# First layer: adjacency pieces loaded at most three ahead of their transposes

## The reference

```python
def _L0_gnn_ref(x, A_shape, W, bias, b):
    y = jnp.linalg.norm(x, axis=-1, keepdims=True)
    A = x @ x.T / (y @ y.T)
    A = A * b
    A = jnp.tanh(A / 8.0) * 8.0
    A = jnp.exp(A) * A_shape
    A = A / jnp.sum(A, axis=-1, keepdims=True)
    x = A @ x
    return x @ W.T + bias
...
x = x + _L0_gnn_ref(_layernorm(x, axis=-1), adj, L0_gnn_W, L0_gnn_bias, L0_gnn_b)
```

## Time and profile before

| | us |
|---|---|
| median of 3 runs | 858.69 |
| lowest and highest | 857.1, 860.33 |
| the profiled execution | 859.55 |
| its span, first to last instruction | 857.8 |
| busy PE, DVE, ACT, POOL in the span | 725.4, 626.7, 450.7, 273.9 |

### The profile page before, as it was taken

One profiled execution on the slowest core, in us unless ns is written; L12 is line 12 of the kernel. 1 busy time (PEld: TensorE's weight loads), 2 busy tenths in 40 slices (PEclk: granted clock), 3 DMA queues, 4 the chain that ended last, 5 costly groups with the idle time before them and its releaser, 6 DMA issues.

```text
span 857.8 us, 15889 instructions
## 1 busy us (share of the span) xinstructions
PE 725.4 (85%) x5287; PEld 550.3 (64%) x5294; DVE 626.7 (73%) x2265; ACT 450.7 (53%) x689; POOL 273.9 (32%) x585
## 2 busy tenths in 40 slices
PE   4799999849999688999999997968678697798893
PEld 2566766529998444777777676755446585787463
DVE  6336656715444468998981799999899999999757
ACT  2366476115555145655653582849687585722153
POOL 4310422555666201112100152142250667770000
PEclk9899999879999899999999998879979898989897
DMA  9999730186887300000000000000000002001001
GB/s 155 193 173 156 136 72 16 40 213 192 231 235 205 118 1 1 1 1 2 2 2 1 1 2 2 2 1 2 0 1 1 2 2 74 26 3 32 1 2 49
DMA packets 82186, 50.37 MB, mean 59 GB/s; under 512 B 42193, under 2 KB 78929, under 8 KB 82097
## 3 DMA queue, kind: packets, MB, share of 16 engines
q1 hardware_dynamic: 64304, 28.35, 15.0%
q0 software_dynamic: 11456, 14.62, 9.1%
q10 hardware_dynamic: 6336, 6.32, 3.1%
HBM read 39.69 MB, written 9.57 MB: 57 GB/s over the span
## 4 chain that ended last, share of the span: by engine, by line
DVE 37%; PE 16%; ACT 5%; issue 5%; DVEq 1%; POOLq 1%; POOL 0%; ACTq 0%
DVE big L1602 6%; DVE cand L1366 5%; DVE cand L1520 4%; PE bank L2145 3%; PE bank L2049 3%; DVE hacc L1515 2%; DVE rm L1360 2%; DVE cand L1541 2%; DVE top L1536 2%; DVE big L1591 2%; PE bank L2128 2%; PE bank L2329 2%; DVE big L1588 2%; PE bank L2342 1%; ACT UT L1861 1%
## 5 line engine op out<-in xcount | busy, mean ns | idle before, releaser
L2128 PE MATMUL bank<-ident,big 128*128 128x128 f32 x512 | 79.6, 304 | 28.4 <-DVEq L1625 19.1
L2128 PEld LDWEIGHTS bank<-ident,big 128*128 128x128 f32 x512 | 61.2, 153 | 54.4 <-DVEq L1625 21.0
L1875 ACT ACTIVATE big<-bank 128x512 f32<-128x512 f32 x128 | 70.4, 597 | 46.6 <-PE bank L2128 46.6
L2049 PE MATMUL bank<-kk,qq 64*128 64x512 f32 x256 | 76.0, 711 | 16.8 <-ACT big L1845 16.2
L2056 PEld LDWEIGHTS bank<-parts,adjT 128*128 128x128 bf16 x1536 | 86.9, 98 | 3.2 <-issue 2.8
L2056 PE MATMUL bank<-parts,adjT 128*128 128x128 bf16 x1536 | 88.2, 219 | 0.1
L1845 ACT ACTIVATE big<-bank,negm 128x2048 f32<-128x2048 f32 x32 | 62.7, 1958 | 48.7 <-DVE fsc L1652 38.4
L1602 DVE SCALAR_TENSOR_TENSOR big<-big,st 128x2048 f32<-128x2048 f32 x32 | 73.9, 2348 | 2.9 <-PE bank L2128 2.9
L572 DVE TENSOR_TENSOR big<-big,adjT 128x1024 f32<-128x1024 f32 x32 | 39.8, 1249 | 48.5 <-ACT big L731 30.8
L428 POOL DMA_INDIRECT ys_scratch<-big,parts x62 | 59.9, 967 | 38.7 <-ACT big L774 28.6
L858 PEld LDWEIGHTS bank<-xrows,big 128*128 128x128 f32 x512 | 62.2, 196 | 14.6 <-DVE big L572 9.7
(11 more groups left out here) (373 smaller groups left out, 1448.1 us busy)
## 6 DMA issues: line engine op xcount, KB each, us to landing
big<-in_L_ffn_w_dram SPq DMA_DIRECT2D x93, 128.0 KB
big<-in_adj_dram POOLq DMA_DIRECT2D x8, 512.0 KB, 9.1
big<-xs_scratch ACTq DMA_DIRECT2D x31, 132.0 KB
kk<-in_adj_dram POOLq DMA_DIRECT2D x4, 512.0 KB, 11.3
qq<-in_adj_dram POOLq DMA_DIRECT2D x4, 512.0 KB, 15.0
xs_scratch<-hacc SPq DMA_DIRECT2D x9, 132.0 KB
xs_scratch<-hacc ACTq DMA_DIRECT2D x8, 132.0 KB
res<-in_x_dram SPq DMA_DIRECT2D x4, 256.0 KB, 5.0
```

The lines of the kernel that those rows point to most:

```text
L1875: nc.scalar.activation(MT[:, 4 * q:4 * q + 4, s * P:(s + 1) * P], bank[:, 5 + q % 2, :].rearrange("p (j i) -> p j i", j=4), ACT.Copy).then ...
L2049: nc.tensor.matmul(bank[:, c, :], qq[lo:lo + DA, (g * G + s) * P:(g * G + s + 1) * P], kk[lo:lo + DA, c * CH:(c + 1) * CH], start=True, st ...
L2128: mm = nc.tensor.transpose(bank[:, 5 + q % 2, j * P:(j + 1) * P], mk[:, s, jt * P:(jt + 1) * P], ident[:, :])
```

## The change

A constant `INFLIGHT = 3` takes the place of the eight slots in POOL's waits: load u waits until piece u - 3 is fully turned. The slots stay eight. Before POOL's next constants only loads 1 and 2 are issued; loads 3 and 4 stand behind these constants, and loads 5 to 15 behind the bias. The piece that is waited for, its semaphore and the count are worked out in the same way as before.

```diff
+        INFLIGHT = 3
...
                     c, q = divmod(u, NC)
-                    if u >= NS:
-                        pool.wait_ge(adj_turned[u % TS], 16 * TPC * ((u - NS) // TS + 1))
+                    if u >= INFLIGHT:
+                        v = u - INFLIGHT
+                        pool.wait_ge(adj_turned[v % TS], 16 * TPC * (v // TS + 1))
...
                 pool.wait_ge(ld_x[NC - 1], 16)
-                for u in range(1, NS):
+                for u in range(1, INFLIGHT):
                     load(u)
...
                 nc.gpsimd.memset(cum[:, 0, :], 0.0).then_inc(consts, 1)
+                for u in range(INFLIGHT, INFLIGHT + 2):
+                    load(u)
                 pool.wait_ge(ld_bias, 16)
...
-                for u in range(NS, NC * NC):
+                for u in range(INFLIGHT + 2, NC * NC):
                     load(u)
```

## The result

| | us |
|---|---|
| the changed kernel, median of 20 runs | 854.78 (849.96 to 862.44) |
| the kernel before beside it, 20 runs | 860.11 (855.42 to 865.68) |
| ratio, 95% interval | 0.9935 (0.9916 to 0.9955) |
| the profiled execution of after, its span | 849.96, 848.2 |

The change gained 0.65%, 5.6 us, against the 7.1 of the prediction. The profile is of the fastest of the 20 executions. The kernel was run twice more, on two chips on which the kernel before takes 875.38 and 873.06 us: there its ratio was 1.0001 and 0.9973, with intervals that include 1. So this is also a case about a gain that every profile of the changed kernel shows at the first gather and that isn't always there at the end.

A forecast was written before the change was run, and what follows sets the result against it. PE was taken as the full engine, idle early because queued loads held back piece 0's transposes. Gains of 4.0 + 2.0 + 1.06 = 7.1 us took 858.7 to 851.6 us; forecast 849.5 to 853.7 (0.68), full range 849.0 to 856.5.

The forecast's parts named there:

- The first piece: Step 1, first chunk: transposes of piece 0 finish without queued loads, product at 22.4 instead of 26.46; PE gains 4.0 us.
- The clock: Step 2, first gather and score: PE's clock stays at 2.4 GHz because its idle time shrinks; gain 2.0 us.
- step 3: First chunk, pairs 2 and 4: pieces 1 and 2 land early, so PE's 0.45 and 0.61 us go; gain 1.06 us.
- The waits of pairs 2 and 4 on transposes: First chunk: pieces 1 and 2 land early, so PE's later waits of 0.45 and 0.61 us go; gain 1.06 us.
- POOL's order: Step 4, POOL's queue: later bias additions and later first scatter cost nothing, their results being needed much later; 0 us.
- The loop of three pieces: Step 5, SP and POOL: about 18 us for three pieces, 6 each, against the consumer's 7.9; no loss.
- the rival's way of losing time: Slower rival, piece 15: loops above 25.4 us make it late; at 27 us a loop, 8 us late, 866.7; chance 0.08.
- the "half" rival: First chunk: piece 0 lands at 24.5 or later, or the clock drops; gain 3 to 5 us, 853.7 to 855.7; chance 0.14.
- the "nothing" rival: First chunk: transposes are slow by themselves, or slow later landings repay the gain; 858.7 within 1 us; chance 0.10.

The follow-up runs named there:

- x_if5: The changed kernel with at most five pieces ahead instead of three (INFLIGHT = 5); 872.78 us, ratio 0.9951 to the kernel before.
- x_fill: The kernel before with 20 idle matmuls ahead of the first gather to keep PE busy; 880.23 us, ratio 1.0042 to the kernel before.
- x_firstbias: The kernel before with load 3 waiting for piece 0 and the bias additions moved behind loads 9 to 12; 873.02 us, ratio 0.9977.
- x_after: The changed kernel run again on a second chip beside the kernel before; 876.07 us, ratio 1.0001.
- y_after: The changed kernel run a third time, on a third chip, beside the kernel before; 872.08 us, ratio 0.9973.
- x_if2: The changed kernel with at most two pieces ahead instead of three (INFLIGHT = 2); 885.15 us, ratio 1.008 to the kernel before.
- x_before: The kernel before, unchanged, run against itself on the second chip; 876.38 us, ratio 1.0012.
- x_bias: The changed kernel with the four bias additions moved behind loads 6 to 9, one each; 870.86 us, ratio 0.993 to the kernel before.
- y_bias: The changed kernel with the four bias additions behind loads 6 to 9, again, on the third chip; 869.75 us, ratio 0.9947 to the kernel before.
- y_small: The changed kernel with each 128 x 512 bias addition split into four of 128 x 128; 873.75 us, ratio 0.9972 to the kernel before.

## Why the prediction was right, and where it was not

1. **The first piece.** Right, by the mechanism named. Product at 22.84 (said: 22.4), and the transposes at their free rate once the load queue was empty. The amount was undercounted: from 21.0 to 22.7 the transpose queue moved 1540 packets, perhaps some of piece 1 among them, where the step had 849 in 0.8 us. The 0.6 us set aside for the report of the last packets covered most of it, and that was luck. The gain on PE was 3.47 of the 4.0 us, because PE's own work ahead of the gather reached to 24.27 instead of 22.99; in the five other profiles with the limit of three from the start the product came at 21.7 to 22.6. x_if5 shows that two loads more undo all of it.
2. **The clock.** Right in what it does here, 2.2 us for 2.0. Wrong as a term by itself: x_fill won it alone and gained nothing. In the sum it stood beside step 3 as if each could be had without the other.
3. **The waits of pairs 2 and 4 on transposes.** Gone, as said. A stop at load 3 alone is not enough for it (x_firstbias).
4. **POOL's order.** This is the step that failed. "Their first reader on DVE stands behind ten products" asked who needs the result of the additions, not what runs beside them. The step had even placed them, "a moment after 28", so from 28 to 34. Pair 2's product could be placed too: 38.27 less the 6 to 7 us of step 3 is about 32. The term set at 0 measured 1.16 us of idle PE in the profile of the result, 4.27 and 1.7 of slow gather in x_after, nothing in y_after: 0 to 6.0 us, by how the first addition lies against the product. The kernel before has the same pair in its traces, POOL's 5.92 us in the earlier trace rows for work that takes 4.93, and I read the row as the cost of the additions. The second half of the step, that the late scatters are asked for two chunks later, met no contrary row; what they may do to everything that runs beside them was not considered, and the stall that goes with the limit is not explained.
5. **The loop of three pieces.** Right: 6.0 us a piece against the 6 worked out, and no product behind the first waits for a transpose in any profile of the changed kernel. At two pieces the loop takes 8.3 us a piece, longer than the consumer, and x_if2 is slower than before; but no product waited for a transpose there either, so the rival's way of losing time showed in no run.

The sum was 7.1 us; the first chunk gave 5.5 in the profile of the result, 6.3 in y_after against x_before (54.72 for 60.98) and 0.4 in x_after. The forecast's own range, 849.5 to 853.7, assumed that a won stretch at the front stays won. With the collision and the stall in the third chunk that isn't so: the three ratios are 0.9935, 1.0001 and 0.9973. The profiles suggest a draw in each execution, but this isn't shown. The executions of the changed kernel spread over 12.5, 13.5 and 10.2 us, those of the kernel before beside them over 10.3, 12.5 and 13.0, and a change that is simply worth more on one chip than on another would give the same three ratios. The measured 854.78 lies in the full range, in the stretch that the "half" rival held; as a difference, the way the sum was made, 5.6 us lie in the forecast's own stretch, 5.0 to 9.2. Either way the range held in part by luck: with the ratio of the second chip the time would have been that of the "nothing" rival, for another reason than that rival gave.

With late additions the kernel beats the kernel before on both chips on which it ran, x_bias with 0.993 and y_bias with 0.9947. That it beats the changed kernel is likely from the profiles but not shown: 0.9947 and 0.9973 on one chip, with intervals that overlap.

## What to carry to other kernels

When a wait is put into a queue, everything behind it moves too: ask for each moved instruction what it will run beside, not only who reads its result, and above all where POOL works on SBUF while DVE has a product of two SBUF operands on the critical path. A DMA queue that is filled early is not free for a second queue behind it: here the transposes ran seven times slower beside queued loads, so load in the order and at the rate of the consumer, with the loop's time checked against it (6.0 us a piece for 7.9 was enough; at 8.3 the last load went out at 127 us instead of 96, and the kernel was slower than before). And a gain early in a kernel is counted only after the same landmarks have been compared further down.

## What the runs showed of the hardware

- A DVE multiplication of 128x1024 with both operands in SBUF and POOL's additions of 128x512 never ran at the same time in the first chunk. One that had started was not interrupted, and the waiting one could miss three boundaries in a row, or a dozen of small additions: 1.22, 1.99, 2.53, 3.39, 4.52 and 5.64 us for the same product (table above), 6.27 with sixteen small additions (y_small). It was not the same side each time that got in.
- POOL's addition of a quarter of the elements took more than a quarter of the time: 0.44 us in the median for 128x128 (y_small), 1.26 for 128x512 (x_after). Four large ones took 4.93 us, sixteen small ones, the same elements, 7.61, of which one was held up by DVE to 1.43.
- In the experiments an idle time of PE of 2.7 to 4.9 us in the first chunk was followed each time by a gather at a lower clock, 2.6 to 3.8 us instead of 1.95; one of 1.16 us was not, in the profile of the result (PEclk 1.00 from 34 to 55), nor one of 2.02 us in x_if2 (2.05 us for the gather).
- Two queues with work share packet by packet over 10 us: 1447 to 1449 (x_firstbias, 34 to 44 us).
